# Spreading eleven row dispatches between tile writes on GpSimd

## What is computed

```python
x = x + gnn(layernorm(x), adj)          # RMS norm, silu, two layers
# the second half, ffn(layernorm(x)):
gate_logits = xf @ Wg + bg
top_w, top_i = top_k(gate_logits, 2)    # two experts for each token
top_w = softmax(top_w)
for e in range(8):
    h = gelu(xf @ W1[e] + b1[e])        # 128 -> 512
    out = out + w_dense[:, e:e+1] * (h @ W2[e] + b2[e])   # 512 -> 128
x = x + out
```

## Time and profile before

| | us |
|---|---|
| median of 3 runs | 490.4 (489.8 to 490.93) |
| the profiled execution, its own time | 493.83 |
| its span, first to last instruction | 492.0 |
| PE busy | 464.5 (94% of the span) |
| DVE / ACT / POOL busy | 337.5 / 305.8 / 299.5 |

### The profile page before, as it was taken

One profiled execution on the slowest core, in us unless ns is written; L12 is line 12 of the kernel. 1 busy time (PEld: TensorE's weight loads), 2 busy tenths in 40 slices (PEclk: granted clock), 3 DMA queues, 4 the chain that ended last, 5 costly groups with the idle time before them and its releaser, 6 DMA issues.

```text
span 492.0 us, 13861 instructions
## 1 busy us (share of the span) xinstructions
PE 464.5 (94%) x3585; PEld 413.7 (84%) x3585; DVE 337.5 (69%) x1438; ACT 305.8 (62%) x942; POOL 299.5 (61%) x276
## 2 busy tenths in 40 slices
PE   8999999999999899797799999999988999999995
PEld 5687777777777568687799999999978999999995
DVE  6787788887876857475666667676556666676662
ACT  5565555666565356454566667777746777677773
POOL 3333767888786575746466566666266656666664
PEclk9999999999999989978999999999999999999998
DMA  6995333323433232333334443432245433333310
GB/s 207 376 319 144 83 93 106 83 87 82 87 86 78 67 76 71 102 95 108 99 101 123 122 136 117 116 104 72 60 124 139 125 101 103 108 102 97 94 33 12
DMA packets 50835, 54.61 MB, mean 111 GB/s; under 512 B 10249, under 2 KB 39474, under 8 KB 50760
## 3 DMA queue, kind: packets, MB, share of 16 engines
q1 hardware_dynamic: 42048, 35.14, 28.1%
q0 software_dynamic: 8240, 18.29, 10.8%
q10 hardware_dynamic: 472, 0.29, 0.2%
HBM read 33.56 MB, written 21.52 MB: 112 GB/s over the span
## 4 chain that ended last, share of the span: by engine, by line
PE 88%; issue 3%; POOL 3%; DVE 2%; DMA 2%; ACT 1%; POOLq 0%; ACTq 0%; another core or an unknown queue 0%; DVEq 0%
PE ps L748 28%; PE ps L766 27%; PE ps L654 11%; PE ps L668 10%; PE ps L741 3%; PE ps L618 3%; PE ps L661 2%; PE ps L628 2%; POOL dispatched_rows L494 1%; PE ps L635 1%; DMA vec_rows<-in_vectors 1%; ACT gelu_t L888 1%; POOL powers L483 1%; DMA eps_col<-in_epsilon 1%; PE ps L644 0%
## 5 line engine op out<-in xcount | busy, mean ns | idle before, releaser
L888 ACT ACTIVATE gelu_t<-ps,block_w 128x128 f32<-128x128 f32 x568 | 164.8, 372 | 55.4 <-PE ps L748 50.6
L766 PE MATMUL ps<-experts,gelu_t 128*128 x1136 | 153.6, 279 | 11.2 <-ACT gelu_t L888 8.6
L748 PE MATMUL ps<-slot_t,block_w 128*128 128x128 f32 x1136 | 154.1, 279 | 6.3 <-ACT gelu_t L888 4.4
L766 PEld LDWEIGHTS ps<-experts,gelu_t 128*128 128x128 f32 x1136 | 139.8, 194 | 14.8 <-issue 14.8
L748 PEld LDWEIGHTS ps<-slot_t,block_w 128*128 128x128 f32 x1136 | 140.8, 194 | 8.1 <-ACT gelu_t L888 4.9
L513 POOL DMA_INDIRECT out_y<-slot_rows x71 | 82.9, 1168 | 58.7 <-DVE slot_rows L1261 41.3
L509 POOL DMA_INDIRECT forwarded_rows<-slot_rows x71 | 81.6, 1149 | 55.0 <-DVE slot_rows L1261 47.2
L1261 DVE SCALAR_TENSOR_TENSOR slot_rows<-ps,slot_rows 128x128 f32<-128x128 f32 x133 | 46.6, 351 | 95.9 <-PE ps L766 54.3
L494 POOL DMA_INDIRECT dispatched_rows<-payload,row_idx x80 | 86.9, 1087 | 28.5 <-issue 17.6
L1152 DVE COPY block_w<-experts 128x644 f32 x142 | 70.6, 497 | 1.3 <-issue 1.3
L814 ACT ACTIVATE hidden<-ps,vec_cols 128x512 f32<-128x512 f32 x64 | 44.0, 688 | 42.0 <-PE ps L654 41.5
(11 more groups left out here) (152 smaller groups left out, 411.4 us busy)
## 6 DMA issues: line engine op xcount, KB each, us to landing
slot_rows<-forwarded_rows SPq DMA_DIRECT2D x63, 131.0 KB
slot_rows<-dispatched_rows SPq DMA_DIRECT2D x79, 67.0 KB
xs<-in_x SPq DMA_DIRECT2D x16, 256.0 KB, 6.6
xs_t<-in_x_t SPq DMA_DIRECT2D x16, 256.0 KB, 5.4
experts<-in_f_w SPq DMA_DIRECT2D x16, 256.0 KB, 4.9
slot_rows<-rrms_rows SPq DMA_DIRECT2D x13, 256.0 KB
adj_in<-in_adj_t SPq DMA_DIRECT2D x16, 128.0 KB, 5.7
dispatched_rows<-payload,row_idx POOLq DMA_INDIRECT x80
```

The costliest lines, as they stand in the source:

```text
L748: mm = pe.matmul(bank((2 * i + c // 2) % FH_BANKS, c % 2 * SLOTS, SLOTS), block_w[:, i % BLOCKS, c * P:(c + 1) * P], slot_t[:, i % 2, :], ...
L766: mm = pe.matmul(bank(Y_BANK + i % 2, 0, P), gelu_t[:, i % 2, c, :], experts[:, bass.ds(at + (OW2 + c * P), P)], start=(c == 0), stop=(c = ...
L888: act.activation(gelu_t[:, i % 2, c, :], ps[:, (2 * i + c // 2) % FH_BANKS, c % 2 * SLOTS:(c % 2 + 1) * SLOTS], ACT.Gelu, bias=block_w[:, ...
```

## The change

Dispatches move on POOL's queue. Group 14's four come out of the graph loop and lose their waits for `fh_done`. They, group 15's four and the last three second choices each go behind every third tile's write: behind the writes of tiles 1, 4, 7, 10 (group 14), 13, 16, 19, 22 (group 15), 26, 29, 32 (second choices). `pow_norms(16)` goes ahead of the write of tile 1. That is eleven dispatches and one power that stand elsewhere. Nothing is added or dropped, and the other engines' instructions keep their order.

```diff
-        LAST_GATE, LAST_RANKS, LAST_FIRSTS = 9, 9, 11
+        LAST_GATE, LAST_RANKS = 9, 9
+
+        FIRSTS_BEHIND = {1 + 3 * n: (G - 2 + n // JT, n % JT) for n in range(2 * JT)}
...
+        SECONDS_BEHIND = {2 + 3 * (2 * JT + n): G - SECONDS_FROM + n
+                          for n in range(SECOND_GROUPS * JT - (G - SECONDS_FROM))}
...
-            for s in range(1, G + 1):
+            for s in range(1, G):
...
-                    if s == G:
-                        pool.wait_ge(fh_done, 6)
                     dispatch(s - 2, 0, 0)
-                    if s == G:
-                        pow_norms(s)
-                        pool.wait_ge(fh_done, 8)
-                    elif live(s + 2):
+                    if live(s + 2):
...
             for i in range(NT):
-                if LAST_FIRSTS <= i < LAST_FIRSTS + JT:
-                    dispatch(G - 1, i - LAST_FIRSTS, 0)
-                if 0 <= (i - RING) // 4 < SECOND_GROUPS * JT - (G - SECONDS_FROM) and i % 4 == RING % 4:
-                    second(G - SECONDS_FROM + (i - RING) // 4)
+                if i == 1:
+                    pow_norms(G)
                 write_tile(i)
+                if i in FIRSTS_BEHIND:
+                    dispatch(*FIRSTS_BEHIND[i], 0)
+                if i in SECONDS_BEHIND:
+                    second(SECONDS_BEHIND[i])
```

More of the change, by code:

```diff
@@ L532, in _ @@
                     second(s - SECONDS_FROM)
-                if s < G:
-                    pow_norms(s)
+                pow_norms(s)
                 if s == 1:
@@ L549, in _ @@
                     dispatch(s - 2, 1, 0)
[L550 to L553, removed]
+                    pool.wait_ge(l2_done, s + 1)
                     dispatch(s - 2, 2, 0)
@@ L559, in _ @@
                     else:
-                        pool.wait_ge(fh_done, 2 if s < G else 12)
+                        pool.wait_ge(fh_done, 2)
                     dispatch(s - 2, 3, 0)
             for i in range(NT):
-                if LAST_FIRSTS <= i < LAST_FIRSTS + JT:
-                    dispatch(G - 1, i - LAST_FIRSTS, 0)
-                if 0 <= (i - RING) // 4 < SECOND_GROUPS * JT - (G - SECONDS_FROM) and i % 4 == RING % 4:
-                    second(G - SECONDS_FROM + (i - RING) // 4)
+                if i == 1:
+                    pow_norms(G)
                 write_tile(i)
+                if i in FIRSTS_BEHIND:
+                    dispatch(*FIRSTS_BEHIND[i], 0)
+                if i in SECONDS_BEHIND:
+                    second(SECONDS_BEHIND[i])
         @block.tensor
```

## The result

The changed kernel takes 495.81 us in the median of 7 runs (494.71 to 498.65), the kernel before on the same chip 490.93 (7 runs, 489.80 to 492.76): a ratio of 1.0111 [1.0087, 1.0136], 4.9 us slower where 4.8 us faster was forecast. The profiled execution took 494.78 us against 493.83 before.

The account below looks back on a forecast made before the run. PE, busy 94%, was taken as the bound, with stalls from POOL's backlog. Losses of 2.9 + 3.9 + 6.4 = 13.2 us instead of 18.0 gain 4.8 off 490.4: 485.6 us, range 479 to 494 for 8 in 10.

Parts of the forecast that it names:

- The step that failed: For the whole change: the same instructions add no work of their own, and only their places change.
- SP's covers for the late landings: SP's loads at tiles 40 and 71: later landings stay hidden, the first by two tiles, 3.8 us.
- The start: Tiles 5 to 8: write 0 goes earlier, POOL's backlog falls to 2.9 us, and 2.9 us are lost instead of 8.3.
- the sign I had set: First 12 tiles: the forecast is wrong if PE idles over 1 us although POOL's backlog is under 3 us.
- The ten dispatches: Dispatches after the first, between tile writes: three cost 3.9 us together and seven cost 6.4 us.
- 1.3: Loss in us for each of three dispatches falling into POOL's run without a pause by tile 12.
- 0.92: Loss in us for each of seven later dispatches, each following on an idle POOL.
- The clock: PE's granted clock, 0.50 from 210 to 216 us, was to stay at 1.00 through 216 us.
- Backlog as the cause of the stalls: First 40 tiles: while POOL issues without a pause, signals between PE and other engines come late; 19.25 us lost.
- The one-to-one of backlog and loss: At the start: loss equals POOL's backlog, as 8.3 us lost beside 8.2, so 2.9 us for 2.9.
- The slower one: Tiles 1 to 34: POOL never catches up, ten dispatches cost 2.1 us each, time 496.3 us; chance 0.24.
- the rival of no change: Stalls at 203, 226, 240 us have another cause than POOL; time stays 490.4 us; chance 0.18.

Follow-up runs that it names:

- round 1: Both kernels run again unchanged, besides two variants of the changed kernel's POOL waits: kernel before 464.32 us, changed kernel 471.49 us, ratio 1.0147.
- `spread24`: All eleven dispatches behind writes up to tile 24, group 14's behind 1, 4, 7, 10, the others packed closer; 488.70 us, ratio 0.9958 to the kernel before.
- `start_only`: Kernel before with only group 14's four dispatches behind writes 1, 4, 7, 10 and the power ahead of write 1; 492.29 us, ratio 0.9935.
- `bounded_dispatch2`: Changed kernel with a bounds check on all dispatches, as the writes have; 496.41 us, ratio 1.0118 to the kernel before.
- `late_memset2`: Changed kernel with a POOL memset added behind the write of tile 138; 498.00 us, ratio 1.0151 to the kernel before.
- `seconds_kept`: Changed kernel with the last three second choices back ahead of writes 16, 20, 24; 496.36 us, ratio 1.0019 to the kernel before.
- `seconds_only`: Kernel before with only the last three second choices moved, behind writes 26, 29, 32; 498.49 us, ratio 1.0109.
- `third_at_32`: Kernel before with only the last second choice moved, from ahead of write 24 to behind write 32; 496.05 us, ratio 1.0123.
- `first_at_32`: Kernel before with only group 15's last first choice moved, from ahead of write 14 to behind write 32; 496.58 us, ratio 1.0111.
- `last_only`: Kernel before with only group 15's four dispatches moved, behind writes 13, 16, 19, 22; 495.05 us, ratio 1.0034.
- `late_dispatch2`: Changed kernel with one second choice sent again behind write 138; 497.82 us, ratio 1.0147 to the kernel before.
- rounds 5 and 1: Round 5: kernel before with its last second choice behind write 28, 471.88 us, or an extra one behind write 80, 467.79 us; kernel before unchanged 464.18 us.
- round 4: Changed kernel with a late dispatch, late memset or bounded dispatches, 496.41 to 498.00 us; change's start alone with late dispatch 492.09; kernel before 489.80.

## Why the prediction was wrong, point by point

**The step that failed** is "The instructions are the same, so their own work adds nothing; only places change". It leaves no term for the program's end. POOL's closing DRAIN is in no busy time and has no place in the expert stage, but it costs by where the last dispatch stands: 7.0 us more behind write 32 than ahead of write 24. This is shown: by one moved DMA alone on either table, by its absence in the kernels whose last dispatch stands at tile 24, and by round 1, in which next to nothing else differs (+7.2 us). What POOL does in the DRAIN stays open. I worked out SP's covers for the late landings and never asked what else reads the order of POOL's DMAs.

**The start** (forecast 2.9 us lost instead of 8.3, a gain of 5.4). Write 0's place was right, POOL caught up at write 4, and tiles 5 to 8 took 7.89 us, inside the 6 to 9 I gave. But 2.0 more are lost ahead of tile 5 (PE waits 1.31 us for ACT at 202.63). From tile 0 to tile 8 it is 19.38 us for eight tiles, 4.2 lost, where before it was 23.57 and 8.4: a gain of 4.2. By the sign I had set, a stall of over 1 us with a backlog under 3 us, the reading behind the number is wrong.

**The ten dispatches and the rest** (forecast 10.3 where now 9.7, a loss of 0.6). From tile 8 to tile 40 the kernel after loses 11.8 us (72.58 less 60.8), before 10.9: a loss of 0.9. Together 3.3 gained in this execution instead of 4.8. Near in size, yet by luck: single losses run up to 2.1, so neither 1.3 nor 0.92 holds for each, and over all the profiles of kernels at 490 us the 40 tiles lose 15.1 to 19.9 us where group 14 is spaced as in the change, and 16.5 to 21.5 where it isn't.

Nor do the medians show the gain. With the growth of the tail taken off, the kernel after gains 2.1 us, `spread24` 1.6 and `start_only` 1.8, but `bounded_dispatch2`, which has the change's order, only 0.4, `late_memset2`, the change and a memset, loses 1.2, and `seconds_kept` loses 2.3. The kernels that move late dispatches alone and leave the start as it was gain as much: `seconds_only` 2.6, `third_at_32` 1.3, `first_at_32` 0.7.

At least some of that is the 1.6 us at the end of the stage (its rows stand at the end of the section on the result): at 490 us the tiles from 137 to 141 take 1.6 us more in `before`, `start_only`, `last_only` and `seconds_kept`, which have POOL's pause ahead of tile 137, than in the kernels with a long tail (leaving out `late_dispatch2`, which has a dispatch there). So a gain from the spacing itself is not shown; `spread24` is the one kernel that is faster than before with all eleven spaced.

**The clock** stayed at 1.00, the level of 2.4 GHz, through 216 us as said. It fell later: its mean is 0.94 from 234 to 240 us and 0.78 from 240 to 246, after PE's idle times of 1.31 and 1.41 us.

**Backlog as the cause of the stalls.** Refuted as a general cause: the kernel before at 464 us has the backlog and no stall. The rule of the Trainium skill that I set against my reading, from "SBUF — State Buffer", section "Who interferes with whom", is nearer to what that trace shows (76.10 us for 40 tiles beside a backlog of 8.0). At 490 us the stalls remain, and in the kernel after they go by single dispatches and not by a backlog: behind each of the first six (199.11, 205.43, 212.60, 219.55, 226.84 and 233.79) a second layer starts 1.0 to 2.1 us late, 3.6 to 4.8 us after the dispatch does, though POOL idles 0.8 to 1.6 us for DVE between them. The one-to-one of backlog and loss, by which the start was costed at 2.9, is thus the second step that failed: the backlog went from 8.2 us to under 3, the loss of the first eight tiles from 8.4 to 4.2. That a dispatch brings the stall fits these rows and was not tested by itself; at 464 us the same dispatches bring none. What makes the stalls appear in some rounds isn't settled.

**The start alone** is open too: `start_only` was 1.8 us faster than its before (494.09), but the same work plus one dispatch, 492.09, was 2.3 slower than its own (489.80). The two medians agree within 0.2; the ones of before don't, and that is 4.3 us between rounds for one kernel. Part of the 2.3 is the extra dispatch's own: in its trace the tiles from 137 to 141 lose 1.4 us more than in `start_only`'s.

**The rivals.** The slower one gave 496.3 and the time is 495.8, but that is luck, its mechanism is wrong: POOL idles by write 4, and the loss is behind the last tile. The chance of 0.24 sat on a number, not on the cause. Its long writes of 1.24 us exist (1.24 in after as well) and decide nothing. Of the rival of no change, that the stalls are not POOL's, the half on the backlog held; it had no term for the end either. **The covers** of SP's loads held: its waits show no landing of a dispatch. DVE waits for a load once in the kernel after, 1.4 us before 357.75, for a slot loaded from `forwarded_rows`; it has no such wait before.

## What to carry to other kernels

Before counting a reorder on POOL as free, look at the program's very end: the time between the last landing and the last instruction, and whose DRAIN fills it. Where it is long, move the last DMA of the other kind (here the dispatches) earlier by a few and read the DRAIN again. And take a stall to a second chip, and at another time, before giving it a mechanism; a term from one profiled execution, when such terms lie up to 5 us apart between kernels with the same start, can't carry a forecast of 5.

## What the runs showed of the hardware

- The tail of POOL's closing DRAIN went with the DMAs that POOL issued behind its last dispatch, up to 113 of them: 5.0 us at 61, 7.7 at 93, 9.0 at 109, 9.3 at 113, which is 0.082 to 0.083 us for each. At 117 and 118 it is 2.0, and POOL has paused for 2.0 to 2.3 us ahead of the 114th. What is counted isn't known.
- A dispatch with three DMAs behind it changed the tail by 0.1 us at most, in a kernel with a long tail and in one with a short; one with 61 behind it set it to 5.0. So the count is not simply one from the last dispatch. Why was not found.
- Every landing had been waited for and the DRAIN still took 8.97 us, so it doesn't wait for the kernel's data. The Trainium skill, "GPSIMD Engine Reference", section "2.1 Instruction dispatch", has each instruction broadcast to eight cores and done when all of them are; whether the DRAIN waits for something those cores put off, no run here shows.
- The same kernel before took 464.2 and 464.3 us in rounds 5 and 1 and 489.8 to 494.1 in the others. In the trace of round 1 the granted clock was 1.00 over the first 40 tiles and they lost 0.1 us. The record gives round 1 (464.3) and round 4 (489.8) the same chip number, 0; if that is the same chip, what differs is its state at the time and not the chip. No run here settles it.
